# Two buffers for the edge-weight gathers in a GAT and R-GCN kernel: even and odd steps, and the weights taken out later in the step

## The reference, cut to what matters

```
seg = edge_type * n + dst
agg = segment_sum(x[src], seg);  cnt = segment_sum(ones, seg)
mean = agg / max(cnt, 1)
h1 = einsum('rni,rio->no', mean, W_rel) + x @ W_root + b_rgcn      # 34 matrices of 768 x 768
xw = h1 @ W_gcn;  deg = segment_sum(ones, dst) + 1;  dinv = rsqrt(deg)
out = segment_sum(xw[src] * (dinv[src]*dinv[dst])) + xw * dinv*dinv + b_gcn
```

## Time and profile before

| what | value |
|---|---|
| median of three executions | 3511.51 us (3502.35 to 3514.48) |
| the profiled execution | 3542.46 us |
| its span | 3540.7 us |
| PE busy | 3228.3 us, 91% of the span |
| DVE, ACT, POOL busy | 2231.7, 1454.1, 1642.5 us |
| granted TensorE clock, mean | 0.966 |

### The profile page before, as it was taken

The page is one execution under the profiler, slowest core; times in us unless marked ns, Lnnn a source line. Parts: engine busy times, 40 slices in busy tenths (PEclk is TensorE's granted clock), DMA queues, the critical chain, the costliest instruction groups (busy, mean ns, idle before and its releaser), DMA issues. The chain is left out here.

```text
span 3540.7 us, 59428 instructions
## 1 busy us (share of the span) xinstructions
PE 3228.3 (91%) x17127; PEld 2000.4 (56%) x17127; DVE 2231.7 (63%) x4605; ACT 1454.1 (41%) x2683; POOL 1642.5 (46%) x1373
## 2 busy tenths in 40 slices
PE   6989999988999999999999999999999988688888
PEld 4544458976555555555556666666666644344545
DVE  8989988779644445444456877778787744322224
ACT  3767747655432333333244545454454521000000
POOL 3720000004556565565424655655566446666661
PEclk9999999998999999999999999999999999789999
DMA  3020011112333333232344655556555544664441
GB/s 90 2 72 0 0 58 74 38 48 76 133 116 102 114 106 123 90 120 97 121 142 142 193 162 172 187 161 197 161 176 168 149 131 133 177 187 132 131 116 56
DMA packets 228620, 411.85 MB, mean 116 GB/s; under 512 B 37764, under 2 KB 177923, under 8 KB 228534
## 3 DMA queue, kind: packets, MB, share of 16 engines
q1 hardware_dynamic: 167664, 268.22, 21.7%
q0 software_dynamic: 60480, 142.01, 15.1%
q10 hardware_dynamic: 390, 0.50, 0.0%
HBM read 259.19 MB, written 151.32 MB: 116 GB/s over the span
## 5 line engine op out<-in xcount | busy, mean ns | idle before, releaser
L2341 PE MATMUL bank<-arena 128*128 128x384 f16 x3675 | 1208.7, 329 | 67.7 <-ACT arena L1214 35.7
L2343 PE MATMUL bank<-arena 128*128 128x384 f16 x3675 | 1206.7, 328 | 6.8 <-issue 6.6
L2344 PE MATMUL bank<-arena 128*128 128x384 f16 x3675 | 1206.7, 328 | 6.3 <-issue 5.7
L1214 ACT ACTIVATE arena<-bank,winv 128x384 f32<-128x384 f32 x700 | 394.9, 579 | 995.4 <-PE bank L2344 863.8
L1821 DVE SCALAR_TENSOR_TENSOR arena<-bank,winv,arena 128x384 f32<-128x384 f32 x525 | 313.4, 613 | 469.0 <-PE bank L2344 383.1
L2341 PEld LDWEIGHTS bank<-arena 128*128 128x128 f16 x3675 | 361.7, 98 | 341.4 <-ACT arena L1214 44.8
L2344 PEld LDWEIGHTS bank<-arena 128*128 128x128 f16 x3675 | 361.8, 98 | 252.0 <-issue 18.1
L2343 PEld LDWEIGHTS bank<-arena 128*128 128x128 f16 x3675 | 362.3, 99 | 241.6 <-issue 20.6
L818 POOL DMA_INDIRECT arena<-y_half,idx_now x360 | 399.4, 1110 | 190.1 <-issue 105.0
L1746 DVE SCALAR_TENSOR_TENSOR arena<-arena,wscale 128x1152 f16<-128x1152 f32 x245 | 368.3, 1539 | 183.1 <-ACT arena L1147 169.1
L805 POOL DMA_INDIRECT w_now<-rel_inv_dram,idx_now x360 | 344.2, 956 | 254.0 <-ACT idx_now L1199 153.1
(11 more groups left out here) (249 smaller groups left out, 4208.4 us busy)
## 6 DMA issues: line engine op xcount, KB each, us to landing
y_half<-arena SPq DMA_DIRECT2D x306, 384.0 KB
arena<-in_L_gnn_W_rel_dram SPq DMA_DIRECT2D x68, 1152.0 KB
arena<-y_half,idx_now POOLq DMA_INDIRECT x720
y_half<-arena SPq DMA_DIRECT2D x34, 294.0 KB
w_now<-rel_inv_dram,idx_now POOLq DMA_INDIRECT x360
cT_dram<-arena SPq DMA_DIRECT2D x1, 5625.0 KB
arena<-cT_dram SPq DMA_DIRECT2D x9, 625.0 KB
arena<-in_x_dram SPq DMA_DIRECT2D x10, 384.0 KB, 9.2
```

The lines of the kernel that those rows point to most:

```text
L1214: nc.scalar.activation(y[half][:, :, c * CQ:(c + 1) * CQ], acc, ACT.Copy, scale=scale).then_inc(r_copied, 1)
L2341: nc.tensor.matmul(acc, h, w_hi[m - 1][:, k, :], start=fresh and k == 0, stop=False, skip_group_check=True)
L2343: nc.tensor.matmul(acc, h, w_lo[m - 1][:, k, :], start=False, stop=False, skip_group_check=True)
L2344: ins = nc.tensor.matmul(acc, l, w_hi[m - 1][:, k, :], start=False, stop=k == KH - 1, skip_group_check=True)
```

## The change

There are two buffers of each kind: `idx_now` and `w_now` for even steps, `idx_odd` and `w_odd` for odd ones. The gathers of odd steps raise other semaphores (`tail_loaded`). Both index buffers are filled before the first step. In a step ACT empties the buffer that was gathered in the step before and fills the index buffer of the same parity for two steps later. The two copies stand no longer behind `m7_out(s, 1)`, but behind `m6_out(s, 3)`, ahead of `m3_out(s, 2)`. The loops of ACT and POOL now hold two steps in a body, and the last three steps with gathers on ACT are written out. The products, the stores, the loads and the second half are as before, but for the counts that the shared semaphores are compared with.

```diff
+        w_odd = sb("w_odd", [P, IDXB, UT], F32)
+        idx_odd = sb("idx_odd", [P, IDXB, UT], I32)
...
+        w_loading = (g_loaded, tail_loaded)
+        w_bufs, idx_bufs = (w_now, w_odd), (idx_now, idx_odd)
...
-            def weights_step(q, i, next_q, next_i):
+            def weights_step(q, i, next_q, next_i, b):
 
                 t4(q, i)
                 pool.wait_ge(idx_copied, i + 1)
                 pool.nop(nofuse=True)
-                weigh(0)
-                weigh(1)
+                weigh(b, 0)
+                weigh(b, 1)
                 t3(next_q, next_i)
...
-            with pool.Fori(1, AGG_PAIRS) as i:
-                weights_step(0, i, 0, i + 1)
+            with pool.Fori(0, AGG_PAIRS // 2) as i:
+                weights_step(0, i * 2 + 1, 0, i * 2 + 2, 1)
+                weights_step(0, i * 2 + 2, 0, i * 2 + 3, 0)
...
                 m7_out(s, 0)
                 m7_out(s, 1)
-                if w is not None:
-                    weights_out(w)
-                if w is not None and q == 0 and (not isinstance(i, int) or i < AGG_PAIRS):
-                    indices_in(w + 1)
                 if e is not None:
                     edge_high(q - 1, e, PER, 1)
...
                 if e is not None:
                     edge_high(q - 1, e, PER, 5)
+                if w is not None:
+                    weights_out(w, half, b)
+                    if more:
+                        indices_in(w + 2, b)
                 m3_out(s, 2)
...
-            indices_in(0)
+            indices_in(0, 0)
+            indices_in(1, 1)
```

More of the change, by code:

```diff
@@ L512, in program @@
         assert UNITS % IDXB == 0 and PER == IDXB and PER % 2 == 0
+        W_USES = [PER // 2 * len(range(b, AGG_PAIRS, 2)) for b in range(2)]
+        w_loading = (g_loaded, tail_loaded)
+        w_bufs, idx_bufs = (w_now, w_odd), (idx_now, idx_odd)
         spread = bank[SUMS][:, 0:P]
@@ L520, in unit @@
         def unit(q, i, m, c):
-            return i * m + (c + q * UNITS), c % 2, i * (m // 2) + (c // 2 + (q + 1) * (UNITS // 2))
+            return i * m + (c + q * UNITS), c % 2, i * (m // 2) + (c // 2 + q * (UNITS // 2) + W_USES[0])
         def tail_slot(i, m, c, t):
@@ L528, in tail_slot @@
             k = c % units * UT + t
-            before = 2 * (UNITS // 2) if k < 2 * UT else 0
+            before = UNITS // 2 + W_USES[0] if k < 2 * UT else W_USES[1]
             return k, (g_loaded + tail_loaded)[k], i * (m // units) + (c // units + before + 1)
@@ L800, in x1_sums, with weigh @@
                 nc.gpsimd.tensor_tensor(s[3], a[:, KH:KT], s[2], ALU.subtract).then_inc(xsum_done, 1)
-            def weigh(c):
+            def weigh(b, c):
                 for t in range(UT):
                     nc.gpsimd.indirect_dma_start(
-                        out=w_now[:, c, t:t + 1], out_offset=None, in_=w_dram,
-                        in_offset=bass.IndirectOffsetOnAxis(ap=idx_now[:, c, t:t + 1], axis=0))\
-                        .then_inc(g_loaded[c % 2 * UT + t], 16)
+                        out=w_bufs[b][:, c, t:t + 1], out_offset=None, in_=w_dram,
+                        in_offset=bass.IndirectOffsetOnAxis(ap=idx_bufs[b][:, c, t:t + 1], axis=0))\
+                        .then_inc(w_loading[b][c % 2 * UT + t], 16)
             def gather(q, i, m, c):
@@ L850, in _ @@
                 if 2 * m < PER:
-                    weigh(2 * m)
-                    weigh(2 * m + 1)
+                    weigh(0, 2 * m)
+                    weigh(0, 2 * m + 1)
             pool.wait_ge(x1_lo, 7 * HT)
@@ L861, in weights_step @@
                 pool.nop(nofuse=True)
-                weigh(0)
-                weigh(1)
+                weigh(b, 0)
+                weigh(b, 1)
                 t3(next_q, next_i)
-                weigh(2)
-                weigh(3)
+                weigh(b, 2)
+                weigh(b, 3)
                 t1_t2(next_q, next_i)
-                weigh(4)
-                weigh(5)
+                weigh(b, 4)
+                weigh(b, 5)
             def rows_step(q, i, e, next_q, next_i, last=False):
@@ L1195, in next_index, with indices_in, weights_out @@
                 nc.scalar.copy(idx_now[:, c % IDXB, :], idx_y[:, bass.ds(u * UT, UT)]).then_inc(idx_next, 1)
-            def indices_in(i):
-                nc.scalar.copy(idx_now.rearrange("p c t -> p (c t)"), idx_w[:, bass.ds(i * (PER * UT), PER * UT)])\
+            def indices_in(w, b):
+                nc.scalar.copy(idx_bufs[b].rearrange("p c t -> p (c t)"), idx_w[:, bass.ds(w * (PER * UT), PER * UT)])\
                     .then_inc(idx_copied, 1)
-            def weights_out(i):
+            def weights_out(w, half, b):
                 for k in range(2 * UT):
-                    act.wait_ge(g_loaded[k], i * (PER // 2 * 16) + PER // 2 * 16)
-                nc.scalar.copy(w_s[:, bass.ds(i * (PER * UT), PER * UT)], w_now.rearrange("p c t -> p (c t)"))\
+                    act.wait_ge(w_loading[b][k], half * (PER // 2 * 16) + PER // 2 * 16)
+                nc.scalar.copy(w_s[:, bass.ds(w * (PER * UT), PER * UT)], w_bufs[b].rearrange("p c t -> p (c t)"))\
                     .then_inc(edge_w, 1)
@@ L1243, in used_high, with one_step @@
                 high(q, i, m, block, ready)
-            def one_step(q, i, next_q, next_i, e, w=None):
+            def one_step(q, i, next_q, next_i, e, w=None, half=None, b=None, more=True):
                 s = step(q, i)
@@ L1344, in _ @@
                 act.wait_ge(x1_stored[i], 16 * 2 * XS0[i])
-            with act.Fori(0, AGG_PAIRS - 1) as i:
-                one_step(0, i + 1, 0, i + 2, None, i)
-            one_step(0, AGG_PAIRS, 0, AGG_PAIRS + 1, None, AGG_PAIRS - 1)
+            with act.Fori(0, (AGG_PAIRS - 2) // 2) as i:
+                for b in range(2):
+                    one_step(0, i * 2 + (b + 1), 0, i * 2 + (b + 2), None, i * 2 + b, i, b)
+            for w in range((AGG_PAIRS - 2) // 2 * 2, AGG_PAIRS):
+                one_step(0, w + 1, 0, w + 2, None, w, w // 2, w % 2, w + 2 < AGG_PAIRS)
             one_step(0, PAIRS - 1, 1, 0, None)
```

## The result

The changed kernel has a median of 3497.85 us in eight executions (3491.89 to 3503.74), against 3510.76 us for eight of the kernel before on the same chip (3502.35 to 3514.48). The ratio is 0.9964, with a 95% interval of 0.9952 to 0.9976: a gain of 12.9 us, real but small. The forecast was 3490. Its profiled execution took 3497.76 us, its span is 3496.0.

A forecast was written before the change was run, and what follows sets the result against it. POOL's own sequence, closed through late signals to ACT and DVE, was taken to set the 56.64 us step. Thirteen steps at 54.8 make 712.4 against 741.2 us, 28.8 less; three quarters, 21.6, gives 3490 us, range 3466 to 3526.

The forecast's parts named there:

- What bounds a step: Steps with gathers: POOL's own sequence sets the step, 56.64 us against 52.14 without gathers, 4.5 us lost by them.
- the hold: News of PE's product ends is held from about 4.5 us into a gather group until about 1 us after its last.
- PE's waits in the step with gathers: Three waits: 0.55 us for an addition, 0.50 amid a product, 2.12 for an eviction; without gathers one of 0.49.
- The first group starts early, `t3` then waits for the load: First gathers start 2.8 us after `t4` instead of 13.51; `t3` then waits some 9 us for the load.
- The load's 9.03 us: Load ahead of `t3` lands 9.03 us after issue, as without gathers, so `t3` starts 21.16 to 21.65 after `t4`.
- The end of the loop: From `t3` to the next `t4`, 33.38 us as before, including 5.68 from the third group's end to `t4`.
- The price at the step's boundary, 1.1 us: First group, moved early, delays `m1` of tile 1 at the step's start: 1.1 us or so, not lengthening the step.
- The slower rival: First group holds `m1` of tile 0, the load is issued late, a step takes 59.3 us: 3541 us; 20%.
- `m6`'s wait under 1.5 us: PE's wait of 2.1 to 2.5 us at `m6` of tile 4 falls under 1.5.
- The first stall: Step 1: `t3` comes at 952.3 instead of 954.57, so PE's 4.35 us wait shrinks by about 2.3.
- Three quarters for plain runs: Plain runs gain three quarters of the profile's 28.8 us, 21.6, as their median lies 31 us below the profiled execution.
- The rival of no change: The hold is the profiler's, or the load comes as late as in step 1 (57.3 us a step): 3511; 24%.

The follow-up runs named there:

- second trace: Kernel before, run again with no edit on the second chip: 3529.28 us, where its median is 3530.41 us.
- the version with the old place: Two buffers as in the changed kernel, but ACT's two copies stay behind `m7_out(s, 1)`: 3517.43 us, ratio 0.9958 to the kernel before.

## Why the prediction was right, and where its steps were off

- **What bounds a step: right on the chip that it was read from.** A step with gathers was 4.5 us longer than one without; leaving the gathers out gave 52.09 us a step and took 68 us from plain runs. The rule of the Trainium skill ("SBUF — State Buffer", section "Who interferes with whom": "PE and ACT never wait on anyone") is about ports. Taken as a rule that ACT never waits for POOL's gathers, it fits the chips without the hold and not those with it.
- **PE's waits in the step with gathers: one was overlooked.** The step of the earlier trace rows has a fourth, of 1.12 us, 4.4 us after `t4`. The four make 4.29 us, against one of 0.49 without gathers; the difference is most of the 4.5 that the step loses.
- **The hold, read as lasting until 1 us after the last gather: too simple.** In the changed kernel `m3` of tile 3 was taken 2.1 us late amid the group, and in the first group evictions came on time up to 9.3 us behind its first gather.
- **The first group starts early, `t3` then waits for the load: right.** The idle time before the first gather is 0.15 us, and `t3` waits 8.5.
- **The load's 9.03 us: the term that was mis-sized.** It takes 10.40. I chose the value without gathers, since the group ends about when the load is issued; but the gathers at the new place are slower (the first took 1.90 us, not 0.96), the group ends 1.9 us after the load's issue, and leaving it out brings 8.95 back. So of the 1.6 to 2.1 us by which `t3` should have come earlier, 0.24 were left in this step (over the steps without the long one, about 0.5). That is why the step is 55.72 us, outside the 54.5 to 55.0 of the forecast.
- **The end of the loop, taken as unchanged: wrong.** It gave 0.66 us, more than the load left. Without the waits in the middle of the step (0.55 and 0.50 us before), and in this step without the one at 4.4 us, PE is ahead: it comes to its last wait 50.3 us after `t4` and not 51.8. `m3` of tile 2 is taken on time, `m3` of tile 3 amid the group, and `m1` of tile 4 1.68 us after the group's end and not 2.33. Together with 0.24 and 0.02 in between that is the 0.92 us between 56.64 and 55.72. That the earlier products are the cause is argued from this and from the version without the first group; no run moved them alone.
- **The price at the step's boundary, 1.1 us: none was seen.** `m1` of tile 0 was taken 8.0 us after `t4`, `m7` of tile 1 was on time at 12.1, and nothing behind them made PE wait. The waits of 1.1 us at 4.4 us after `t4` are not this price, since they stood there before. The slower rival did not come. Why the delay is so small in this group was not tested; its gathers are longer and less even than those of the others.
- **`m6`'s wait under 1.5 us: wrong.** It is 2.69 in this step, and 33.7 us over thirteen steps as against 33.8.
- **The first stall: not as told.** The sum counts 2.3 us for a shorter wait in the first step. The kernel before had a first step of 56.57 us in its second trace, and the version with the old place one of 60.55, so this stall comes and goes between executions.
- **The copies at no cost: right** as far as plain runs can tell. **The second half unchanged: not settled,** as said above.
- **Three quarters for plain runs: luck.** I laid the 31 us between profile and median to the profiler; they belonged to that one execution. The traces' thirteen steps gave 17.6 us, the plain runs 12.9, with an interval of about 8 to 17, and this looks like three quarters. But without the first step the traces give 1.1 us a step, 14.4 for thirteen, close to the plain runs. The forecast of 21.6 us came out nearer than the full 28.8 because a factor that was not there made up for part of a load term that was too small.
- **The rival of no change** was wrong in its mechanism, but it is what happens on the other chips.

What stays open: what the hold is, why two chips have it and the others not, and whether a pause prevents it. The last was tried in five runs and never met such a chip.

## What to carry to other kernels

When two stretches of a program do the same work and differ in length, the difference bounds what any edit to the odd part can win; find it before looking at idle times, of which 153 us here were worth 13. When a wait is removed, the next one in the same engine's list inherits most of it, and the moved work may lengthen the very transfer that is waited for. A trace explains the chip that it was taken on: before a mechanism of signals or contention is built upon, the kernel should be timed on a second chip.

## What the runs showed of the hardware

- On two chips, with eight gathers in a row on POOL, ACT and DVE took PE's products late. In the changed kernel's third group a product that ended 5.0 us behind the first gather was taken at once, one at 6.4 us 2.1 us late, one at 7.9 us 3.5 us late, which was 1.7 us behind the group's end. The longest delays, in the second group of the kernel before, were 5.1 to 5.8 us, in twelve steps of thirteen. In the first group at its new place evictions were on time up to 9.3 us behind its first gather.
- On the later chips nothing of it appeared in the steps of the first half: the same gathers ran, and a step had 52.1 us, as on the second chip without gathers (52.09).
- The whole kernel before took 3354 to 3358 us there against 3511 and 3530, a difference of 4.5% and more between chips with one program. The late signals in the first half explain only part of it. The changed kernel's two traces have spans of 3496.0 and 3352.8 us: of the 143 us between them 47 lie in the thirteen steps, 21 in the second half's fifteen (61.2 against 59.8 us each), and 77 behind the last `t4` (663.4 against 586.2 us). Why the chips differ there is open.
- So in the second half the chips differ by 1.4 us a step in the changed kernel, less than in the first half. There a step on the later chips took 59.87 us with hardly any spread, against 59.3 to 64.2 in the second trace of before.
- Gathers that begin beside DVE's `low` take 1.90 and 1.54 us for the first two and not 0.96, on both kinds of chip. In the changed kernel's traces the load issued while that group runs lands in 9.6 to 10.7 us, and in 8.8 to 9.3 us in the versions without the group.
